# One more K/V gather in each later turn of the edge loop, in place of an x tile gathered early and projected in the loop

## The reference

```
q = (x @ Wq.T + bq).reshape(n, H, HD)
k = (x @ Wk.T + bk).reshape(n, H, HD)
v = (x @ Wv.T + bv).reshape(n, H, HD)
score = clip(einsum('ehd,ehd->eh', q[dst], k[src]) / sqrt(HD), -10, 10)
ex = exp(score - segment_max(score, dst)[dst])
alpha = ex / segment_sum(ex, dst)[dst]
wv = segment_sum(alpha[:, :, None] * v[src], dst)
x1 = x + wv @ Wp.T + bp
h = layernorm(x1, ln_g, ln_b)
h = gelu(h @ W1.T + b1) @ W2.T + b2
out = layernorm(x + x1 + h)
```

## Time and profile before

| | before |
|---|---|
| median of 3 runs | 1381.24 us (1381.17 to 1381.86) |
| the profiled execution's own time | 1384.61 us |
| its span, first to last instruction | 1382.7 us |
| mean granted TensorE clock | 0.875 of full speed |
| busy: PE, DVE, ACT, POOL | 79%, 69%, 49%, 54% |
| K/V gathers, x gathers | 750, 32 |

### The profile page before, as it was taken

One profiled execution on the slowest core, in us unless ns is written; L12 is line 12 of the kernel. 1 busy time (PEld: TensorE's weight loads), 2 busy tenths in 40 slices (PEclk: granted clock), 3 DMA queues, 4 the chain that ended last, 5 costly groups with the idle time before them and its releaser, 6 DMA issues.

```text
span 1382.7 us, 25384 instructions
## 1 busy us (share of the span) xinstructions
PE 1095.3 (79%) x6188; PEld 703.5 (51%) x6188; DVE 954.5 (69%) x1539; ACT 673.4 (49%) x1936; POOL 750.6 (54%) x800
## 2 busy tenths in 40 slices
PE   8987777877778868878777868878878877787897
PEld 6843344544545545545454545545445544455565
DVE  6836777677677666677667767667767767676773
ACT  3222344545545545554654544554564563563542
POOL 3556565555565555565565655555655655555500
PEclk9986878898989988897989888988988998988899
DMA  9977877777877777777777777777777786777710
GB/s 330 330 254 235 284 222 243 231 213 226 254 218 234 241 214 212 240 221 234 230 229 235 228 236 211 232 221 232 230 227 223 228 255 195 229 237 223 215 57 25
DMA packets 154884, 312.23 MB, mean 226 GB/s; under 512 B 32199, under 2 KB 73125, under 8 KB 154790
## 3 DMA queue, kind: packets, MB, share of 16 engines
q0 software_dynamic: 61536, 200.85, 48.7%
q1 hardware_dynamic: 93254, 110.43, 25.3%
HBM read 270.02 MB, written 41.16 MB: 225 GB/s over the span
## 4 chain that ended last, share of the span: by engine, by line
issue 27%; PE 23%; SPq 18%; another core or an unknown queue 14%; ACT 9%; DVE 7%; DMA 1%; ACTq 0%; DVEq 0%
SPq L623 5%; PE quad L866 5%; PE bank L482 5%; SPq L616 3%; DVE kv L1627 3%; DVE score L1614 2%; PE bank L921 2%; PE bank L968 2%; PE bank L942 2%; SPq L661 1%; SPq L579 1%; PE quad L933 1%; SPq L635 1%; ACT hid L490 1%
## 5 line engine op out<-in xcount | busy, mean ns | idle before, releaser
L400 POOL DMA_INDIRECT kv<-kv_rows,src_sb x750 | 713.9, 952 | 518.4 <-issue 190.2
L1607 DVE TENSOR_TENSOR prod<-kv,quad 128x1024 f32<-128x1024 f32 x196 | 239.2, 1221 | 233.3 <-remote 106.2
L482 PE MATMUL bank<-hT,w_sb 128*128 128x256 f32 x736 | 225.1, 460 | 26.0 <-ACT hid L490 26.0
L1627 DVE TENSOR_TENSOR kv<-kv,bank 128x1024 f32<-128x1024 f32 x196 | 237.9, 1214 | 7.9 <-ACT kv L1200 4.8
L1614 DVE TENSOR_REDUCE score<-prod 128x32 f32<-128x1024 f32 x196 | 237.5, 1212 | 0.8
L482 PEld LDWEIGHTS bank<-hT,w_sb 128*128 128x128 f32 x736 | 168.1, 234 | 64.2 <-ACT hid L490 16.8
L502 PE MATMUL bank<-w_sb,hid 128*128 128x256 f32 x736 | 193.7, 417 | 0.0
L942 PE MATMUL bank<-kv,onehot 128*32 128x264 f32 x1568 | 140.7, 434 | 37.6 <-ACT acc_sb L1214 22.8
L502 PEld LDWEIGHTS bank<-w_sb,hid 128*128 128x128 f32 x736 | 151.1, 211 | 29.3 <-issue 6.8
L921 PE MATMUL bank<-staged,place 128*128 128x264 f32 x196 | 81.8, 504 | 101.6 <-ACT staged L1208 86.7
L490 ACT ACTIVATE hid<-bank,b_sb 128x256 f32<-128x256 f32 x184 | 77.3, 471 | 169.2 <-PE bank L482 64.7
(11 more groups left out here) (163 smaller groups left out, 1405.6 us busy)
## 6 DMA issues: line engine op xcount, KB each, us to landing
qwin<-q_rows SPq DMA_DIRECT2D x392, 64.0 KB
dst_rows<-edge_dstT SPq DMA_DIRECT2D x50, 256.0 KB
q_rows<-q_next SPq DMA_DIRECT2D x25, 512.0 KB
kv_rows<-kv_out SPq DMA_DIRECT2D x24, 512.0 KB
kv<-kv_rows,src_sb POOLq DMA_INDIRECT x750
agg_rows<-acc_sb SPq DMA_DIRECT2D x98, 82.5 KB
xT_sb<-xT SPq DMA_DIRECT2D x25, 256.0 KB, 5.3
xq_sb<-xT SPq DMA_DIRECT2D x25, 256.0 KB
```

Source lines behind the costliest of these rows:

```text
L400: return nc.gpsimd.indirect_dma_start(out=rows, out_offset=None, in_=kv_dram, in_offset=bass.IndirectOffsetOnAxis(ap=index, axis=0))
L482: last = nc.tensor.matmul(bank[:, j * SB:(j + 1) * SB], w1_sb[:, k * HIDDEN + f * P:k * HIDDEN + (f + 1) * P], hT[:, k], start=(k == 0), s ...
L1607: nc.vector.tensor_tensor(prod[:, slot % 2].rearrange("p (i c) -> p i c", c=C), kv[:, slot, :, 0:C], quad[:, :, 0:C], ALU.mult).then_inc(s ...
L1627: nc.vector.tensor_tensor(kv[:, slot, :, C:2 * C].rearrange("p i (h d) -> p i h d", d=HD), kv[:, slot, :, C:2 * C].rearrange("p i (h d) -> ...
```

## The change

`X_TURN` becomes the number of turns, so no turn has an x tile in slot 7, and the lists `x_turn` and `x_tiles` answer alike for the turns written out and for the looped ones. The ten x tiles of the first turns stay.

```
-    X_TURN = 2 if LOOPED else TURNS
+    X_TURN = TURNS
...
 def x_turn(turn):
-    return not isinstance(turn, int) or X_TURN <= turn < LOOP_FROM + 2 * LOOPED
+    return X_TURN <= (turn if isinstance(turn, int) else LOOP_FROM) < LOOP_FROM + 2 * LOOPED
...
 def x_tiles(turn, i):
     if not isinstance(turn, int):
-        return (X_TILE,) if i == X_SLOT else ()
+        return x_tiles(LOOP_FROM, i)
     return tuple(t for u, b, t in X_TILES if (u, b) == (turn, i))
```

## The result

The changed kernel takes 1408.34 us (median of 4 runs, 1407.14 to 1411.77), the kernel before 1381.55 us on the same chip: ratio 1.0176, 95% interval 1.0140 to 1.0211, or 26.8 us more (by the interval 19 to 29). The profiled execution took 1407.78 us, with a span of 1406.0.

What follows compares the result with a forecast made beforehand. POOL's chain of gathers and the stops between its runs were taken to bound the kernel; 27.5 + 4.8 - 6.6 = +25.7 us on the median 1381.24 gave 1407 us, range 1380 to 1420.

Steps and rivals of the forecast that it cites:

- 22 gathers, issue and short gaps: On POOL, 22 added gathers cost 1.25 us each from start to start: +27.5 us.
- longer runs +4.8: On POOL, each added gather lengthens the stop ending its run: 22 x 0.22 = +4.8 us, bounds 0 and 4.8.
- relief -6.6: Without ACT's copy L1248, slot 7's product starts earlier, shortening PE-late stops: 0.30 us a turn, -6.6, bounds 0 and -28.6.
- The long run: POOL's run from slot 6's tile 2 to slot 0's tile 1 becomes one gather longer; the residual still starts behind it.
- The 0.22 us a gather: PE's signals take effect after POOL's run, later by some 0.22 us a gather: stops 1.89 behind four, 2.55 behind seven.
- about 52.3 us: Forecast time of one turn of the loop after the change, where it took 51.
- the 1.86 us: PE work delaying the second feed-forward matrix (986.40 - 984.54); its removal hidden by POOL's run, uncovered worth 41 us at most.
- 2.37 as the most: Twelve L502 on PE at 1.2 GHz take 2.37 us more a turn; taken as hidden, 0.
- PE as the bound: Rival: PE's list sets the turn, the first L502 starts 1.86 us earlier: -13.4, 1368 us; chance 0.14.
- The absorbed gather: Rival: a PE-late stop, 1.30 us above its floor, takes in the added gather: 1381 to 1384 us; chance 0.09.
- each gather carries its share of the stops: Rival: the turn's stops go with the number of gathers, 1.64 us each: +36, 1417 us; chance 0.11.
- the clock: Rival: PE's lower clock after idling comes through, slot 7's q rows ending after 991.91: 1433 us and more; chance 0.04.

Runs made afterwards that it cites:

- run 5: The changed kernel unaltered, measured once more on the chip of other runs: 1395.56 us against 1374.23 for the kernel before, ratio 1.0182.
- run 9: Kernel before with its x tile kept, one or three further gathers a turn left out (22 or 66 in all): 1370.06 us, ratio 0.9877; 1332.48 us, ratio 0.9615.
- run 1: Kernel before without the steps of the loop's 22 x tiles on PE, ACT and DVE, 31 gathers a turn kept: 1368.81 us against 1370.21, ratio 0.9972.
- run 2: Changed kernel with the x tile's PE and ACT steps put back on other data, result unused: 1392.48 us, ratio 1.0142 to the kernel before.
- run 6: As the kernel before without the loop's x tile steps, but leaving out slot 3's fourth gather instead of slot 7's: 1372.15 us, ratio 1.0000 to the kernel before.
- run 4: Changed kernel with a small POOL fill (128x8) between slot 7's second and third gathers, inside the run of eight: 1395.17 us, ratio 1.0145 to the kernel before.
- run 10: Changed kernel with a long POOL fill (128x1024) in the run of eight: 1403.84 us against 1383.56 for the kernel before, ratio 1.0135.
- run 11: Kernel before with the long POOL fill (128x1024) between slot 7's second and third gathers, in its run of seven: 1399.14 us against 1383.95, ratio 1.0085.

## Why the prediction was right

*The sum.* Forecast 1407 us, measured 1408.34; 25.7 us more were forecast, and 26.8 by the medians, 23.2 by the profiled executions came. That it came within 1.1 us is in part luck: the interval is 19 to 29 us, and the changed kernel's loss on another chip was 25 (19 to 31, run 5). Term by term, from the two traces:

| | forecast | measured |
|---|---|---|
| 22 gathers, issue and short gaps | +27.5 | +28.3 |
| stops: longer runs +4.8, relief -6.6 | -1.8 | -3.4 |
| head and tail | 0 | -1.6 |

*The long run* is there as named, eight gathers and the residual tied to their end. The 0.22 us a gather that I took from runs of four to seven was too much for the eighth: 2.61 against 2.55, 0.06 in the turns shown, 0.14 by the medians. The relief is not by shorter stops where PE is late, as I had put it (what they take beyond the usual hardly changed, run 9), but by five stops fewer (151 to 146); their mean went from 2.17 to 2.22 us. So the two small terms of the sum, +4.8 and -6.6, were not right one by one, and that they nearly cancel is luck; the term that carries the forecast is the issue and gap of the gathers. A turn was to take about 52.3 us where it took 51; it takes 52.1 where it took 51.1.

*PE's part.* L448 stands 0.14 us behind the residual (1004.30 against 1004.16) where it stood 1.86, so 1.72 of the 1.86 us came, and gave nothing that the time shows (run 1). Part was given back at once: twelve L502 took 4.24 us in place of 2.86, at a granted clock of 0.66, between the levels of 1.2 and 2.4 GHz, behind 5.82 us of idle PE. Over the kernel L502 grew from 193.7 us (736 products, mean 417 ns, in the kernel before) to 215.7, 1.0 us a turn, where I had set 2.37 as the most. The Trainium skill (TensorE: Matmul & The Clock Gate, What's actually happening) says that activity releases the throttle; the trace agrees in that the products behind the emptier stretch have a granted clock of 0.66 and those behind the fuller one 1.00. That it would not show in the time was the forecast, and runs 1 and 2 bear it out within their intervals.

*The rivals.* PE as the bound (1368 us) falls with runs 1 and 2. The absorbed gather falls with the result. That each gather carries its share of the stops (1.64 us) is not what was measured, 1.22 us (0.9 to 1.3). One point I had not seen: for gathers taken away the price is 0.8 (run 9), since PE's lateness takes part of the issue back, and for one added beside the x tile's work it is 0.9 (0.6 to 1.2, run 2). The intervals overlap, so no run shows that the price differs between adding and taking away, nor that the 1.25 us of issue is always paid in full.

*What was shown and what not.* That the gather makes most of the loss, and not the x tile's removal, is what runs 1 and 2 show; that its place or the clock has no part in it holds within the intervals of runs 1, 2, 5 and 6. That PE's signals take effect late during a run is shown by runs 4 and 10 for the residual: same work, a fill of 0.12 us or 0.98 us, and 5.6 or 2.25 us of wait. The semaphore records show it for the whole loop, and that no transfer was waited for there. Why a run of gathers holds them stays open, and so does what part of the loop's time this holding makes, since the break in runs 10 and 11 brought no net gain.

## What to carry to other kernels

An engine that issues gathers can set the time at 54% busy: count issue, gap and stop together, and ask whether the stops go with the runs or with the engine waited for. Work that is taken off engines which stand in a wait is worth almost nothing (here some 95 us of PE's and 25 of ACT's for 4), while one more instruction on the chain of issues costs most of its step or all of it: 0.8 to 1.2 us here, of 1.25. Before a price is carried over from one run to another, look at its interval: these three, 0.8, 0.9 and 1.2, cannot be told apart.

## What was not expected of the hardware

A fill of 0.12 us between two gathers is free, since it lies in the 0.30 us gap, and one of 0.98 us costs 0.82. During a run of gathers PE's signals come late, up to 7.3 us behind the modelled end of the work here, while ACT's and DVE's do not bunch behind the runs (140 of 420 and 79 of 367 fall into stops, against 379 of PE's 490). A break of about 1 us lets one of PE's through in the middle of a run, and on balance the kernel gains nothing by it. The kernel before takes from 1370 to 1384 us from chip to chip, a spread half as large as the change, so only ratios on one chip were compared.
